# VectorE turns first-layer rows in 32-column squares, four transfers scatter them to DRAM, and odd slots send turned maxima ahead of query parts

## What is computed

```python
q, k, v = hidden @ Wq + bq, ctx @ Wk + bk, ctx @ Wv + bv
scores = einsum('bkgld,bksd->bkgls', q, k) * scale + mask
out = einsum('bkgls,bksd->bkgld', softmax(scores), v) @ Wo + bo
x = out + hidden
hidden = (x - mean(x)) * rsqrt(var(x) + 1e-6) * gamma + beta
```

## Time and profile before

| | |
|---|---|
| Median of 3 runs | 1800.2 us (1799.7 to 1803.21) |
| The profiled execution | 1802.59 us, its span 1800.8 us |
| PE busy | 1729.5 us, 96% |
| VectorE (DVE) busy | 1251.8 us, 70% |
| ScalarE (ACT) busy | 1057.7 us, 59% |
| GpSimd (POOL) busy | 585.8 us, 33% |
| DMA packets | 224986, 235.88 MB, mean 131 GB/s |
| Mean granted clock of TensorE | 0.986 of 2.4 GHz |

### The profile page before, as it was taken

One profiled execution on the slowest core, in us unless ns is written; L12 is line 12 of the kernel. 1 busy time (PEld: TensorE's weight loads), 2 busy tenths in 40 slices (PEclk: granted clock), 3 DMA queues, 4 the chain that ended last, 5 costly groups with the idle time before them and its releaser, 6 DMA issues. The chain is left out here.

```text
span 1800.8 us, 35959 instructions
## 1 busy us (share of the span) xinstructions
PE 1729.5 (96%) x11009; PEld 1022.4 (57%) x11009; DVE 1251.8 (70%) x1680; ACT 1057.7 (59%) x2402; POOL 585.8 (33%) x1165
## 2 busy tenths in 40 slices
PE   5899999999999999999999999999999999999996
PEld 3465566565566565566565555565565565565542
DVE  6476776677776677776677776677776776776774
ACT  1465666666666566665566665565665655665653
POOL 2132332333332333332333332333332333332321
PEclk8899999999999999999999999999999999999998
DMA  8455544454554454554444554454544454544421
GB/s 281 121 154 140 145 131 122 135 142 125 145 139 119 132 143 129 146 138 128 128 143 127 143 129 105 128 131 115 140 124 105 124 136 119 134 114 122 129 86 42
DMA packets 224986, 235.88 MB, mean 131 GB/s; under 512 B 73738, under 2 KB 199940, under 8 KB 224164
## 3 DMA queue, kind: packets, MB, share of 16 engines
q1 hardware_dynamic: 204452, 205.82, 41.9%
q10 hardware_dynamic: 20480, 29.38, 6.9%
HBM read 101.39 MB, written 22.02 MB: 69 GB/s over the span
## 5 line engine op out<-in xcount | busy, mean ns | idle before, releaser
L750 DVE TENSOR_REDUCE mx<-ms 128x2 f32<-128x750 f32 x896 | 819.6, 930 | 479.8 <-PE ms L877 474.1
L616 ACT ACTIVATE probs<-sc 125x448 f32<-125x448 f32 x1536 | 750.5, 541 | 305.5 <-PE sc L848 298.9
L848 PE MATMUL sc<-qs,ks 99*125 99x448 bf16 x1536 | 445.8, 362 | 24.1 <-DMA qs<-mT 15.6
L877 PE MATMUL ms<-ks,qs 96*128 96x375 bf16 (+1 forms) x2560 | 439.0, 325 | 17.4 <-DMA qs<-qp 10.5
L848 PEld LDWEIGHTS sc<-qs,ks 99*125 99x125 bf16 x1536 | 189.9, 136 | 256.0 <-ACT probs L616 142.9
L898 PE MATMUL pv<-probs,vs 125*32 125x448 f32 x3072 | 321.6, 552 | 0.0
L877 PEld LDWEIGHTS ms<-ks,qs 96*128 96x128 bf16 (+1 forms) x2560 | 176.9, 98 | 193.3 <-issue 55.0
L940 PE MATMUL job<-wo,on 128*112 128x512 f32 x512 | 264.2, 598 | 5.7 <-POOL on L525 5.7
L965 PE MATMUL job<-xT,wq 128*128 128x224 f32 x1024 | 216.2, 354 | 0.9 <-ACT qf L656 0.9
L764 DVE RECIPROCAL orec<-osum 128x112 f32<-128x112 f32 x256 | 214.5, 840 | 0.9 <-DMA osum<-oraw 0.9
L624 ACT COPY oraw<-pv 128x448 f32<-128x448 f32 x128 | 68.1, 532 | 243.1 <-PE pv L898 243.1
(11 more groups left out here) (54 smaller groups left out, 957.9 us busy)
## 6 DMA issues: line engine op xcount, KB each, us to landing
ctxT<-in_ctxT SPq DMA_DIRECT2D x64, 750.0 KB, 6.0
qs<-qp SPq DMA_DIRECT2D x768, 56.0 KB, 2.8
ks<-kp SPq DMA_DIRECT2D x768, 46.9 KB, 2.7
osum<-oraw ACTq DMA_DIRECT2D x128, 112.0 KB, 2.9
oc<-oraw ACTq DMA_DIRECT2D x128, 112.0 KB, 3.4
mask<-in_mask SPq DMA_DIRECT2D x64, 164.1 KB, 3.1
xT<-in_xT SPq DMA_DIRECT2D x32, 224.0 KB, 3.4
xin<-in_x SPq DMA_DIRECT2D x32, 224.0 KB, 6.2
```

The costliest lines, as they stand in the source:

```text
L616: nc.scalar.activation(probs[0:KCS, k, j, :], sc[j][0:KCS, 0:GL], ACT.Exp)\
L750: nc.vector.tensor_reduce(mx[o][:, cols], ms[n % 2][:, :, 0:S2], AX_X, ALU.max).then_inc(max_done[o], 1)
L848: last = nc.tensor.matmul(sc[j][0:KCS, 0:GL], ks[p][0:KM, g, rows], qs[p][0:KM, g, :], start=True, stop=not masked)
L877: last = nc.tensor.matmul(to, qs[o][0:KT, group, cols], ks[o][0:KT, group, :], start=True, stop=not masked)
```

## The change

`yT` becomes [128, 16, 32]: 16 blocks of 32 columns, each holding squares of 32 x 32. One VectorE instruction (`turned_rows`, piece 6) transposes each 32 x 32 square of `y` in place of PE's four transposes and ScalarE's copy. `y` gets 128 partitions, the last 32 set to zero at the start (rows 96 to 111 are written over by each result). Since the squares are turned but not moved, `store_yT` issues four transfers, one for each 32 rows; each writes, for 32 partitions and 16 blocks, 32 columns (the last one 16) to their places in `yT_mid`, whose layout is now [feature, row]. The load of `xT` reads the same 448-byte pieces as before from it.

The schedule: in odd slots the second maximum of piece 5 goes to piece 4; values are projected in pieces 4, 5 and 6 in both layers (in the first layer they were in 4 and 5); the first query copies go from piece 4 to 5. SP's queue sends mT in odd slots after query part 0 and before parts 1 and 2, as in even ones. The second layer's rows `bo`, `gamma` and `beta` are loaded at the end of slot (1, -1) instead of in slots (1, 0), (0, 1) and (1, 1).

```diff
-STEPS_AT = [[1, 1, 1, 1, 1, 1, 1, 1, 1, 1, 1, 1], [0, 1, 1, 1, 1, 2, 1, 1, 1, 1, 1, 1]]
+STEPS_AT = [[1, 1, 1, 1, 1, 1, 1, 1, 1, 1, 1, 1], [0, 1, 1, 1, 2, 1, 1, 1, 1, 1, 1, 1]]
-VALUES_AT = [[{1: (0, 1), 2: (2,)}, {1: (0, 1), 2: (2,)}], [{4: (0, 1), 5: (2,)}, {4: (0,), 5: (1,), 6: (2,)}]]
+VALUES_AT = [{1: (0, 1), 2: (2,)}, {4: (0,), 5: (1,), 6: (2,)}]
-QUERY_PARTS_AT = [7, 4]
+QUERY_PARTS_AT = [7, 5]
-    yT_d = nc.dram_tensor("yT_mid", (B, P, DC * S), F32, kind="Internal").ap()
+    yT_d = nc.dram_tensor("yT_mid", (B, D // SQ, SQ, S), F32, kind="Internal").ap()
-        y = two(sb, "y", [S, D])
-        yT = sb("yT", [P, DC, S])
+        y = two(sb, "y", [P, D])
+        yT = sb("yT", [P, D // SQ, SQ])
...
                 sp.wait_ge(yT_ready[p], made)
-                sp.dma_start(yT_d[b], yT[:, :, :].rearrange("p a b -> p (a b)")).then_inc(yT_out[p], 16)
+                for q in range(SQUARES):
+                    rows = slice(SQ * q, min(SQ * q + SQ, S))
+                    sp.dma_start(yT_d[b][:, :, rows].rearrange("a p l -> p a l"),
+                                 yT[SQ * q:SQ * q + SQ, :, 0:rows.stop - rows.start]).then_inc(yT_out[p], 16)
...
                     stack_terms(p, 0, qs[p], qp, 0, of=(0,))
-                    if p == 1:
-                        sp.wait_ge(q_p2[p], queries)
-                        stack_terms(p, 0, qs[p], qp, 0, of=(1,))
-                if a_ok and p == 1:
-                    max_rows(o, 0, count(2 * ahead + 1))
-                if a_ok and p == 0:
+                if a_ok:
                     max_rows(o, 0, count(2 * ahead + 1))
                 if j_ok:
-                    if p == 0:
-                        sp.wait_ge(q_p2[p], queries)
-                        stack_terms(p, 0, qs[p], qp, 0, of=(1,))
+                    sp.wait_ge(q_p2[p], queries)
+                    stack_terms(p, 0, qs[p], qp, 0, of=(1,))
                     sp.wait_ge(q_p3[p], queries)
                     stack_terms(p, 0, qs[p], qp, 0, of=(2,))
...
+                if first_values(p, i):
+                    load_rows(1, w_in[1])
...
-                def rows_out():
-                    act.wait_ge(t_ps[p], stored + 1)
-                    if not isinstance(stored, int) or 2 * stored + p > 0:
-                        need(act, yT_out[o], 16 * (stored + p))
-                    nc.scalar.copy(yT[:, :, :].rearrange("p a b -> p (a b)"), pv[:, 0:GL])\
-                      .then_inc(yT_ready[p], 1)
...
+                def turned_rows():
+                    dve.wait_ge(y_ready[p], stored + 1)
+                    if not isinstance(stored, int) or 2 * stored + p > 0:
+                        need(dve, yT_out[o], 16 * SQUARES * (stored + p))
+                    nc.vector.transpose(yT[:, :, :].rearrange("p a b -> p (a b)"), y[p][:, :]).then_inc(yT_ready[p], 1)
...
+                        if k == TURNED_AT[p] and step == 0 and s_ok and lay[4] == 0:
+                            turned_rows()
...
                             pe.wait_ge(v_ready[u], n + 1)
-                            if s_ok and lay[4] == 0:
-                                pe.wait_ge(yT_ready[p], stored + 1)
-                            elif j_ok:
+                            if j_ok:
                                 pe.wait_ge(k_evac[p], proj + 1)
...
-                    def transpose_rows():
-                        if j_ok:
-                            pe.wait_ge(k_evac[p], proj + 1)
-                        elif p_ok:
-                            pe.wait_ge(pv_evac[o][1], post + 1)
-                        pe.wait_ge(y_ready[p], stored + 1)
-                        for t in range(DC):
-                            last = nc.tensor.transpose(pv[:, S * t:S * t + S], y[p][:, P * t:P * t + P], ident[0:S, 0:S])
-                        last.then_inc(t_ps[p], 1)
```

More of the change, by code:

```diff
@@ L19 @@
 P = 128
+SQ = 32
 DC = D // P
@@ L26 @@
 LOWEST = -3.0e38
+SQUARES = -(-S // SQ)
 UNITS = LAYERS * B // PAR
@@ L262, in cross_attention_two_layers @@
         o_ps = two(sem, "o_ps")
-        t_ps = two(sem, "t_ps")
+        y_pad = sem("y_pad")
         mt_ps = two(sem, "mt_ps")
@@ L324, in load_xT @@
                 b, before = batch(p, n, layer), count(2 * n)
-                turned = count(16 * (n - PER) + 16) if layer == 1 else 0
+                turned = count(16 * SQUARES * (n - PER) + 16 * SQUARES) if layer == 1 else 0
                 need(sp, q_ps, before)
                 need(sp, yT_out[p], turned)
-                src = xT_d if layer == 0 else yT_d
-                sp.dma_start(xT[:, :, p, :], src[b].rearrange("p (a b) -> p a b", a=DC)).then_inc(xT_in[p], 16)
+                if layer == 0:
+                    src = xT_d[b].rearrange("p (a b) -> p a b", a=DC)
+                else:
+                    src = yT_d[b].rearrange("(a q) p l -> (q p) a l", a=DC)
+                sp.dma_start(xT[:, :, p, :], src).then_inc(xT_in[p], 16)
             def load_x(p, n, layer):
@@ L344, in store_y @@
                 dst = y_d if layer == 0 else out
-                sp.dma_start(dst[b], y[p][:, :]).then_inc(y_out[p], 16)
+                sp.dma_start(dst[b], y[p][0:S, :]).then_inc(y_out[p], 16)
             def store_yT(p, n):
@@ L460, in next_layer @@
                     load_wo(1, w_in[1], slice(2, NG))
-                if (p, i) in ((1, 0), (0, 1), (1, 1)):
-                    load_row(ROWS[2 * i + p - 1][0], 1, ROWS[2 * i + p - 1][1], w_in[1])
             load_wk(0, w_k)
@@ L679, in slot @@
                         k_out()
-                    if k == TURNED_AT[p] and s_ok and lay[4] == 0:
-                        rows_out()
                     if k in QUERIES_AT[p] and QUERIES_AT[p][k][-1] % 2 == 1 and j_ok:
@@ L721, in _ @@
             last.then_inc(consts, 1)
+            for p in range(PAR):
+                nc.vector.memset(y[p][S // SQ * SQ:P, :], 0.0).then_inc(y_pad, 1)
+            dve.wait_ge(y_pad, PAR)
             dve.wait_ge(w_q, 16 * NQ)
@@ L737, in slot @@
                 o = 1 - p
-                plain = 0 if s_ok and lay[4] == 0 else 1
                 if first_values(p, i):
@@ L791, in result_rows @@
                     need(dve, y_out[p], 16 * stored)
-                    if not isinstance(stored, int) or 0 < stored <= PER:
-                        need(dve, t_ps[p], stored if lay[4] == 0 else PER)
-                    nc.vector.scalar_tensor_tensor(out=y[p][:, :], in0=zg[:, :], scalar=rstd[:, 0:1], in1=beta[lay[4]][:, :],
+                    nc.vector.scalar_tensor_tensor(out=y[p][0:S, :], in0=zg[:, :], scalar=rstd[:, 0:1], in1=beta[lay[4]][:, :],
                                                    op0=ALU.mult, op1=ALU.add).then_inc(y_ready[p], 1)
+                def turned_rows():
[3 more added lines that the diff above has]
+                    nc.vector.transpose(yT[:, :, :].rearrange("p a b -> p (a b)"), y[p][:, :]).then_inc(yT_ready[p], 1)
                 for k in range(PIECES):
@@ L804, in slot @@
                             deviation()
-                        if k == max(VALUES_AT[p][plain]) and step == 0 and a_ok:
+                        if k == max(VALUES_AT[p]) and step == 0 and a_ok:
                             values()
@@ L994, in slot @@
                             max_columns(p, 1, main)
-                        if k in VALUES_AT[p][plain] and a_ok:
-                            project_values(VALUES_AT[p][plain][k])
-                        if k == TURNED_AT[p] and s_ok and lay[4] == 0:
-                            transpose_rows()
+                        if k in VALUES_AT[p] and a_ok:
+                            project_values(VALUES_AT[p][k])
                         if k in QUERIES_AT[p] and j_ok:
```

## The result

The changed kernel takes 1808.18 us (median), the kernel before, run beside it, 1802.17 us. The ratio is 1.0035 with an interval of 1.0018 to 1.0052: slower, by 6.0 us of the medians or 6.3 by the ratio. The forecast was 11.9 us slower, on 1800.2. The direction holds, the size is half. The profiled executions are 3.3 us apart (spans 1804.1 and 1800.8 us); that of after lies 2 us under its median, so medians decide what follows, and profiles say where. TensorE's mean granted clock is a part of the gap: 0.987 in the profile of after, 0.9845 on average over its 20 executions, and 0.9867 over 79 executions of the kernel before that ran beside the experiments (0.986 in its profile).

A forecast was written before the change was run, and what follows sets the result against it. PE, busy 96% of the span, was taken as the bound, with SP's odd-slot queue right behind. Transposes -9.6, first-layer stalls +23.5 and second-layer gain -2 made +11.9 on 1800.2: 1812 us, range 1788 to 1830.

The forecast's parts named there:

- Part 1: Transposes off PE, copy on ScalarE included: 0.6 us less per first-layer pair, 9.6 us over 16 pairs.
- Part 2: VectorE's turn in odd-slot piece 6: 0.75 us, costed at nothing because the moved second maximum hides it; 24 us if not.
- Part 3: One store becomes four on SP's odd-slot queue: 0.61 us per issue, as xT's load, delaying everything behind by 1.35 us.
- my bounds of 0.5 and 2.0: Queue delay in us from the four stores, with issues at 0.39 us or at 0.78 us each.
- the step that I named: Second layer: mT's waits go, but the last query part limits the gain to 0.28 us; some seven pairs give 2 us.
- My own formula for the stall: First-layer wait for the last query part at the next even slot's start: 1.47 us in 16 pairs, 23.5 us.
- Part 4: mT ahead of two query parts in odd slots: in the first layer it stays put, the last part comes 1.35 us later.
- the remaining edits: Later first query copies, values spread as in the second layer, earlier row loads: nothing, within 1 us.
- A: Rival, chance 0.24: SP's queue keeps up, issues at 0.39 us, parts landing in 2.9 instead of 3.5 us; 1789 us.
- B: Rival, chance 0.13: issues at 0.39 us, landings as now; sum -1.7, so 1798 us, no change.
- C: Rival, chance 0.10: PE's clock drops after a third of 16 stalls, 5 x 1.7 = 8.5 us more; 1820 us.
- D: Rival, chance 0.11: the scatter to DRAM is slow, VectorE's turn waits for the previous store; 42 us more, 1854 us.

The follow-up runs named there:

- steps back: Changed kernel with the second maximum of odd slots in piece 5 again, as before: 1807.6 us, 1.0031 of the kernel before.
- schedule only: Kernel before with the new step table, value pieces, query copies, mT order and row loads, transposes still on PE: 1798.6 us, ratio 0.9984.
- turn only: Changed kernel with the step table, value pieces, query copies, mT order and row loads of before: 1803.6 us, 1.0019 of the kernel before.
- stores moved: Changed kernel with the odd slot's four stores issued in the even slot before it, behind its key parts: 1794.3 us, 0.9953 of the kernel before.
- mT last again: Changed kernel with query part 1 put before mT in odd slots: 1817.0 us, 1.0076 of the kernel before.
- copies back: Changed kernel with the first query copies of odd slots in piece 4 again: 1804.3 us, 1.0015 of the kernel before.
- four plain stores: Changed kernel storing the yT tile as it lies, in four transfers of 32 partitions, rows in wrong places: 1803.2 us, 0.9997 of the kernel before.
- xT layout: Changed kernel with input xT laid out in DRAM so both sides of its load have the same three dimensions: 1800.0 us, ratio 0.9985.
- all of it: Changed kernel with stores in the even slot, matching xT input, earlier xT and ctxT loads, and ScalarE's odd-slot outputs in piece 11: 1756.0 us.

## Why the prediction was right, and where its sizes were off

**What bounds the kernel** held. PE with SP's odd-slot queue right behind it fits the runs: what shortens the queue or the landings helps, what takes VectorE's cover away (steps back) doesn't hurt.

**Part 1, transposes**: -0.6 us a pair forecast, -0.54 measured as PE's busy time. The number is right and its reading isn't shown: the second layer, which has no transposes, fell by 0.40 too ((638.63 - 633.82) / 12). The ten first-layer pairs of "schedule only" and of "turn only" are:

```profile
267.80:808.80 541.00, 533.03 (x3481) 322.17 (x3480) 384.19 (x521) 334.19 (x760) 182.34 (x360) 1.00 0.50 133
278.30:824.60 546.30, 530.67 (x3400) 312.76 (x3400) 392.72 (x540) 325.04 (x740) 181.56 (x362) 1.00 0.54 132
```

With the new tables and the transposes a pair has 53.30 us of work, 0.06 less than before; with the turn and the old tables 53.07, 0.29 less. I had put the whole difference between the layers down to the transposes, though their odd slots also spread the values differently. What the transposes alone take stays open between some 0.1 (0.54 - 0.40) and 0.5 us (53.30 - 52.82); in time the nearest comparison, "stores moved" against "schedule only", gives 4 us in all, not 9.6.

**Part 2, the turn**: 0.75 us taken, 0.697 measured, hidden as said. But the cover that I named, the moved maximum, isn't what hides it: with the steps back the time is the same.

**Part 3, the stores.** This is the term that was mis-sized. I took 0.61 us for an issue, since xT has the same dimensions and count; it is 0.37, with the registers for the address some 0.55 from one to the next (2.01 us for four). So the delay is 0.7 us, not 1.35; it lay within my bounds of 0.5 and 2.0. What makes xT's issue dear is not its count of pieces but that its two sides differ in form: with the same form on both sides it costs 0.41 us from `yT_mid` and 0.43 from the input. That this is the rule is inferred from these three transfers. The consequence for the second layer I missed altogether: its load from the new `yT_mid` is cheaper by 0.2 us, twice a slot, and the last part is issued at +22.23 instead of +22.75. The gain there is 4.3 us over twelve pairs where I had 2, and not by the step that I named: mT's waits do go (8.3 to 0.2 us), but those for query parts come in their place (1.5 to 11.5), and what fell is PE's busy time. How the gain divides between this and the order of mT stays open: "schedule only", with the order alone, has 0.44 us a pair, "turn only", with the cheaper load alone, 1.06, and after, with both, 0.36, for its last part takes 3.90 us to land instead of 3.47 and 3.19.

**The landing.** I held it at 3.5 us before and after. On average it is 3.32 before and 3.81 after in the first layer, and mT's goes from 3.60 to 4.64. My own formula for the stall, 0.1 + 0.1 + delay - 0.08, with 0.68 of queue and 0.49 of landing gives 1.29 us; PE's idle time of a pair grew by 1.69 - 0.40 = 1.29. I had 1.47. So two errors, one of twice the delay and one of no change in landing, nearly cancelled, and the first-layer pair came out at 54.5 where I said 54.6. That is luck, and so is part of the 1.29: the formula knows the last part's wait alone, while over half of the waiting is for mT. A right number for a stretch is no proof of its terms.

**Part 4, the order of mT**: that mT stays about where it was is right (+21.65 to +21.08), and "mT last again" shows what the order is worth with the new tables, 8.8 us. Probably wrong is the sentence that the remaining edits cost nothing within 1 us ("copies back" is 4 us faster than after, but the intervals overlap; "steps back" 0.6): they bring ScalarE's outputs from +22.05 to +21.18 in a first-layer slot, among the last transfers of the queue. Copies back brings them to +21.67 and steps back to +21.50, so each of the two edits does a part.

**The sum.** Forecast -9.6 + 23.5 - 2 = +11.9. By the profile -8.6 (16 x 0.54) + 20.6 (16 x 1.29) = +12.0 for sixteen pairs like the ten measured, and -6.4 for the second layer and the end: +5.6. The real stretches up to the second layer make +9.7 (-0.3, +7.5 and +2.5), and with -6.4 the +3.3 of the spans. Against the forecast (-9.6 + 23.5 = 13.9 and -2) each part is over 4 us lower; that is why the size in the profile is under a third. The +6.0 of the medians is nearer to the forecast through a term that the sum had at nothing, the clock.

**The rivals.** A and B asked for issues of 0.39 us. That came true, and yet the time isn't theirs (1789 and 1798), since both let the landings stay or shrink, and the four delay the queue by 0.7 us and not by 0.5. C, the clock, is half borne out. Its price was right (1.7 us, from "stores moved"). In the profiles it comes once between 200 and 1700 us before (from 1355.66) and once after (from 1094.00), right behind a wait like this one of after:

```profile
1095.84 0.33 PE L879 MATMUL ms<-ks,qs 96*128 96x375 bf16 x1 [2.07 <-DMA qs<-qp]
```

But this profile is one of the fullest clocks of its kernel. Over the executions after has 0.9845 and before 0.9867. A slot like that at 433.39 takes 0.05 x 31.24 / 1800 = 0.0009 off the mean for 1.7 us, so 0.0022 are two to three more such slots, an estimated 4 us; and among the 20 executions of after a line fitted through time and clock gives 2.0 us for each 0.001. So more than half of the 6 us goes with a lower clock, and C's five slots were two to three too many. That the longer waits bring the clock down is what the single slots show, not these averages. D, a slow scatter: the four land in 1.9 us (2.0 before), no wait of VectorE for the store appears, and four plain stores keep the pairs. The Trainium skill says that transfers under 512 B are read, changed and written back (DMA: Bandwidth & Descriptors, Specifications). The trace shows a small price at most: the scattered transfers (three of 64 KB, one of 32) land in 1.9 us (median), the plain ones of 56 KB in 1.6. D's 1854 us is far off.

**Left open**: how exactly two transfers of ScalarE and one of 750 KB delay a part of 56 KB. The runs show that moving them moves the landing; that they share DMA engines with it is the plain reading, but no row names the engine of a packet that waited. Landings of single profiles differ by some 0.3 us between kernels with the same queue, so smaller differences in the table's last column say nothing.

## What to carry to other kernels

When work is moved off the bounding engine onto another one, count the DMA issues that come with it and the queue in front of which they stand: here four issues at the head of a full queue cost up to 14 us and turned a gain of 8 into a loss of 6, and issuing them in the other slot, whose queue has room, brought the 8 back. For a transfer that is waited for, look at what else is in flight as it is issued, on every queue: one number that let two 112 KB outputs leave after it was worth 29 us, more than the whole change. And before a lower busy time is put down to an edit, look at a stretch that the edit doesn't touch: here the second layer's fell nearly as much. A wait can also cost more than its length, when the clock falls behind it; compare the mean granted clock of many executions, not of the one that was profiled.

## What the runs showed of the hardware

- The issue of a transfer on SP's queue with three dimensions took 0.37 to 0.43 us (medians; after and "xT layout") where both sides have the same form and 0.61 to 0.64 us (before and after) where they differ.
- Four stores of 512 pieces of at most 128 bytes to DRAM landed in 1.9 us each (median); four plain ones of 56 KB, with the same bytes in all, in 1.6 us ("four plain stores"), one store of 224 KB in 2.0 us (before).
- VectorE turned 16 x 4 squares of 32 x 32 in f32 in 0.697 us.
- A part of 56 KB landed in 2.3 us with nothing large issued just before it ("all of it") and in 3.6 to 4.2 us behind a load of 750 KB and two stores of 112 KB (the kernels from after to "xT layout"; averages over first-layer odd slots).
- After waits of 1.5 to 2.1 us (PE, slots from 433.39 in "stores moved" and 1094.00 in after) the granted clock of the slot was 0.95 and 0.94, and the slot took 1.7 us more of PE work (29.63 against 27.94, "stores moved").
